# Moving the next group's first layer norm and step-size chain in among the matrix steps of a fused state-space and expert kernel

## The reference, cut to what matters

```python
x = x + attn(layernorm(x))     # a recurrence over the tokens, 4 heads
x = x + experts(layernorm(x))  # router, top 2 of 8 experts, and a shared one

# inside attn, for the tokens t in order:
dt    = clip(softplus(dt_raw + dt_bias), 1e-4, 0.1)
denom = 1 + dt * kdamp + dt**2 * A
v = (v - dt*A*y + dt*u*Bv) / denom
y = y + dt*v + dt*u*By
o = y . Cy + v . Cv
```

## Time and profile before

| what | us |
|---|---|
| median of 3 runs | 531.29 (530.99 to 531.33) |
| the profiled execution | 531.18 |
| its span, first to last instruction | 529.4 |
| DVE busy | 445.4 (84%) |
| PE busy | 446.4 (84%) |
| POOL busy | 282.7 (53%) |
| ACT busy | 242.6 (46%) |

### The profile page before, as it was taken

How to read it: one execution, slowest core, us unless ns; L and a number is a source line. 1 busy time by engine, 2 the same in 40 slices (tenths; PEclk the granted TensorE clock), 3 DMA queues, 4 the chain that set the end, 5 groups by cost and what they waited for, 6 DMA issues and landing times.

```text
span 529.4 us, 9508 instructions
## 1 busy us (share of the span) xinstructions
PE 446.4 (84%) x3185; PEld 344.8 (65%) x3185; DVE 445.4 (84%) x1268; ACT 242.6 (46%) x482; POOL 282.7 (53%) x367
## 2 busy tenths in 40 slices
PE   6980159996989989997889969898789969998997
PEld 5360158774756667675757659676656658876986
DVE  7699988968999999968999998968889998787542
ACT  1522227443475436442575526443466534343463
POOL 2007887656108876657108686567305776777000
PEclk9686559999999979999999988999899998998999
DMA  7500000200000001200000000110000000000000
GB/s 221 169 1 0 1 1 2 81 2 1 0 1 1 1 1 43 80 2 2 1 0 2 0 2 21 47 36 2 1 0 2 1 1 22 1 2 1 1 11 11
DMA packets 14794, 10.23 MB, mean 19 GB/s; under 512 B 1797, under 2 KB 13966, under 8 KB 14618
## 3 DMA queue, kind: packets, MB, share of 16 engines
q1 hardware_dynamic: 14746, 9.63, 6.2%
HBM read 8.55 MB, written 1.07 MB: 18 GB/s over the span
## 4 chain that ended last, share of the span: by engine, by line
DVE 41%; PE 37%; POOL 9%; issue 8%; ACT 3%; DMA 1%; SPq 0%; DVEq 0%; POOLq 0%; ACTq 0%
PE BC L612 6%; DVE tpA L1291 6%; DVE GV L1291 5%; DVE xr L1439 5%; PE HB L515 4%; DVE BC L1302 4%; PE GV L634 4%; POOL vt L1628 3%; PE HB L572 3%; PE HB L504 3%; POOL rinv L1663 2%; DVE mm L1339 2%; DVE GV L1302 2%; PE HB L622 2%; PE OO L693 2%
## 5 line engine op out<-in xcount | busy, mean ns | idle before, releaser
L612 PE MATMUL BC<-xnT,winT 128*128 128x128 f32 x512 | 78.8, 303 | 40.7 <-ACT pr L926 22.8
L612 PEld LDWEIGHTS BC<-xnT,winT 128*128 128x128 f32 x512 | 69.3, 211 | 54.1 <-issue 28.9
L1625 POOL TENSOR_TENSOR big<-mm 128x256 f32<-128x256 f32 x64 | 50.2, 784 | 52.3 <-DVE mm L1339 45.7
L1648 POOL TENSOR_SCALAR uT<-uT,skipT 128x512 f32<-128x512 f32 x8 | 12.5, 1570 | 89.3 <-DVE w L1424 53.9
L564 PE MATMUL HB<-xnT,w 128*128 128x512 f32 x108 | 52.0, 603 | 3.7 <-ACT gtm L1013 2.1
L1628 POOL TENSOR_TENSOR vt<-mm 128x256 f32<-128x256 f32 x64 | 53.9, 842 | 0.0
L634 PE MATMUL GV<-big,vt 128*128 128x128 f32 x256 | 44.0, 296 | 8.9 <-POOL vt L1628 8.9
L1637 POOL TENSOR_TENSOR mm<-ab,pr 128x256 f32<-128x256 f32 x48 | 41.4, 884 | 14.9 <-ACT pr L926 14.9
L950 ACT ACTIVATE big<-GV 128x256 f32<-128x256 f32 x60 | 23.1, 384 | 56.8 <-PE GV L637 55.5
L1337 DVE TENSOR_TENSOR mm<-BC,pr 128x512 f32<-128x512 f32 x64 | 44.2, 691 | 5.7
L634 PEld LDWEIGHTS GV<-big,vt 128*128 128x128 f32 x256 | 35.4, 200 | 16.8 <-POOL vt L1628 13.6
(11 more groups left out here) (212 smaller groups left out, 1117.1 us busy)
## 6 DMA issues: line engine op xcount, KB each, us to landing
ab<-dt_rows SPq DMA_DIRECT2D x12, 256.0 KB, 4.2
xr<-in_x SPq DMA_DIRECT2D x4, 256.0 KB, 4.9
winT<-in_w_inT SPq DMA_DIRECT2D x1, 1024.0 KB, 6.5
w<-in_rw SPq DMA_DIRECT2D x1, 1024.0 KB
out<-xr SPq DMA_DIRECT2D x3, 256.0 KB, 3.0
taps<-in_dw_wT SPq DMA_DIRECT2D x1, 512.0 KB, 3.8
w<-in_sw SPq DMA_DIRECT2D x2, 128.0 KB
out<-xr SPq DMA_DIRECT2D x2, 128.0 KB, 1.8
```

The costliest lines, as they stand in the source:

```text
L612: last = pe.matmul(b[:, j * TS:(j + 1) * TS], winT[:, col:col + NS], xt, start=True, stop=True)
L1625: pool.tensor_tensor(wt[q % 8][:], m[:, 0], m[:, 3], ALU.add)
```

## The change

The preparation of group g+1 up to dt squared leaves the head loop. On DVE it becomes `front_stage(g + 1, slot)`, called from `between`: one instruction (in two slots, two) at a time among the steps of group g. A dependent instruction takes its wait (`behind`) in its own slot. The other engines get their parts at fixed places between the experts. The rows and the four denominator products stand at the front of the head loop, in iterations 0, 1, 2 and 4 in place of 9, 10, 12 and 13. The running sums stay at 16 and 17. Group 0's own preparation, ahead of everything, stays as it was.

```diff
-DENS_AT = (9, 10, 12, 13)
+F_DENS, DENS_AT = (9, 10, 12, 13), (0, 1, 2, 4)
+SCANS_AT = (16, 17)
+S_STATS, S_AGGR, S_EPS, S_LOGITS, S_DT = 0, 4, 6, 32, 52
+XN_AFTER, XNT_AFTER, LOGITS_AFTER = 2, 3, 4
+DT_OPS = 12
...
 # tensor
+            norm_T(LN1, 1)
+            logits(1)
             pe.wait_ge(ab_done, 1)
...
             for g in range(NG):
+                if g + 1 < NG:
+                    rows_of_dt(g + 1)
                 for k in range(STEPS_OF[g]):
...
-                        front_early(g + 1, k)
+                        if k in DENS_AT:
+                            denominator(g + 1, DENS_AT.index(k))
...
                         hidden(g, e)
+                        if g + 2 < NG:
+                            if e == XNT_AFTER:
+                                norm_T(LN1, g + 2)
+                            if e == LOGITS_AFTER:
+                                logits(g + 2)
                         if e:
                             expert_out(g, e - 1)
...
 # scalar
             for n in range(CHUNKS):
                 convert(0, n)
+                if n == 0:
+                    norm1(1)
+                if n == 1:
+                    xnT_copy(1)
+                if n == 2:
+                    logits_copy(1)
+                if n == 4:
+                    step_exp(1)
             for g in range(NG):
+                if g + 1 < NG:
+                    rows_copy(g + 1)
...
                         for n, last in CONV_AFTER:
                             if e == last:
                                 convert(g + 1, n)
+                                if n == 5 and g + 2 < NG:
+                                    step_exp(g + 2)
+                        if g + 2 < NG:
+                            if e == XN_AFTER:
+                                norm1(g + 2)
+                            if e == XNT_AFTER:
+                                xnT_copy(g + 2)
+                            if e == LOGITS_AFTER:
+                                logits_copy(g + 2)
...
 # vector
+            def front_stage(g, slot):
+
+                if S_STATS <= slot < S_STATS + GT:
...
+                    ins = dve.bn_stats(stats[:, c, :], xr[g % 3][:, c, :])
...
+                if S_AGGR <= slot < S_AGGR + 2:
...
+                if slot == S_EPS:
+                    behind()
+                    dve.tensor_scalar(mv[:, :, 1], mv[:, :, 1], EPS_LN, None, ALU.add).then_inc(ln_var, 1)
+                if slot == S_LOGITS:
...
+                if slot == S_LOGITS + 2:
+                    behind()
+                    dve.tensor_scalar(lx, lx, 0.0, None, ALU.min).then_inc(dt_e, 1)
+                n = slot - S_DT
+                if n == 0:
+                    dve.wait_ge(dt_exp, g + 1)
+                    chained(dve.tensor_scalar(le, le, E_MAX, None, ALU.min))
...
 # gpsimd
             def fills(g):
-                skip_gate(g)
+                if g == 0:
+                    skip_gate(g)
+                if g + 1 < NG:
+                    scale_and_shift(ln_index(LN1, g + 1))
+                if g:
+                    skip_gate(g)
```

More of the change, by code:

```diff
@@ L477, in norm_T, with logits @@
                 last.then_inc(h_ready, 1)
-            def front_early(g, k):
+            def logits(g):
+                pe.wait_ge(h_free, h_read_of("xnT", g))
+                hb = h_bank("logits", g)
+                for c in range(GT):
+                    last = pe.matmul(hb[:, NH * c:NH * c + NH],
+                                     xnTs[g % 2][:, HALO + c * TS:HALO + (c + 1) * TS],
+                                     winT[:, COL_DT:COL_DT + NH], start=True, stop=True)
+                last.then_inc(h_ready, 1)
@@ new lines, in rows_of_dt, with denominator @@
+            def rows_of_dt(g):
+                pe.wait_ge(dt_done, g + 1)
+                hb = h_bank("rows", g)
+                for c in range(GT):
+                    last = pe.transpose(hb[0:2 * NH, c * TS:(c + 1) * TS],
+                                        dtts[g % 2][:, c].rearrange("p i h -> p (i h)"), ident[:])
+                last.then_inc(h_ready, 1)
+            def denominator(g, h):
+                pe.wait_ge(h_free, h_read_of("rows", g))
+                hb = h_bank("den", g, h)
+                pe.matmul(hb[:], coef8[:, h, :], rows8, start=True, stop=True).then_inc(h_ready, 1)
@@ L480, in front_early, with front_first @@
+            def front_first(k):
                 if k == F_XNT:
-                    norm_T(LN1, g)
+                    norm_T(LN1, 0)
                 if k == F_LOGITS:
[L484 to L489, removed]
@@ L490, in front_early @@
-                    last.then_inc(h_ready, 1)
-                if k == F_ROWS:
[L493 to L504, removed]
+                    logits(0)
@@ L834, in _, with norm1 @@
             by_tile = lambda t: t.rearrange("p (c t) -> p c t", c=GT)
[L836 to L846, removed]
-                if k == F_XNT:
[L848 to L854, removed]
+            def norm1(g):
+                act.wait_ge(ln_rstd, ln_index(LN1, g) + 1)
+                act.wait_ge(h_ready, USE[("xnT2", g - 2) if g >= 2 else ("xnT", g - 1)] + 1)
+                for c in range(GT):
+                    last = act.activation(xn[:, c, :], xr[g % 3][:, c, :], ACT.Identity, bias=shift[:, c:c + 1],
+                                          scale=rstd[:, c:c + 1])
+                last.then_inc(ln_xn, 1)
@@ L1028, in _ @@
             for k in range(MID_STEPS):
[L1029 removed]
+                front_first(k)
             head_powers()
@@ L1452, in between @@
                     add_expert(g - 1, e, c)
+                if g + 1 < NG and slot < 2 * DS:
+                    front_stage(g + 1, slot)
             dve.memset(ones[:], 1.0)
```

138 lines of the change are left out of this document (101 added, 37 removed).

## The result

The changed kernel takes 553.87 us (median of 6, 547.84 to 556.20) against 531.31 for the kernel before, measured beside it: a ratio of 1.0371, interval 1.0302 to 1.0441. I had forecast slower, but 537.0 with a range up to 543. The profiled execution has a span of 552.9 us and a mean granted clock of 0.901, against 529.4 and 0.932.

The account below looks back on a forecast made before the run. DVE was taken to bound group 1's steps, and PE, with DVE close behind, the head loops. Steps pay 18.6 us, loops gain 12.7: 5.9 more than 531.2 gives 537.1, stated as 537.0, range 533 to 542, whole range 527 to 543.

Parts of the forecast that it names:

- What the head loop gains: Head loops of groups 0 to 2: preparation leaving them gives back 1.7, 5.0 and 6.0 us, 12.7 in all.
- the 48 us that I had named as a sign of being wrong: Head loops: forecast near 46 us; one under 45 or over 48 would show the prediction wrong.
- ceiling of 47.4: Head loop: the last group's 44.2 us plus products 1 to 3 at 1.05 us each.
- PE's own sum: Head loop: PE busy 46.28 less 1.9, 44.4 us, plus some 1.5 of waiting, said to agree with 46.0.
- What the step stages pay: Steps of groups 0 to 2: slots, waiting and contention cost 4.6, 7.0 and 7.0 us, 18.6 in all.
- contention of DVE with POOL's fills: Steps: each chain instruction waits for a fill's end; 2.8 us for eight in group 0, 1.3 each in groups 1 and 2.
- wait at slot 52: Steps of groups 1 and 2: DVE waits 3.5 us for ACT's exponential, after PE idles 2.6 us before the transposes.
- rival 3: Step stage: PE's clock falls after the new 2.6 us gap, costing PE 3 us; two groups give 543; chance 0.10.
- The cover: Before pair 0: rows on PE and their copy on ACT cost nothing, hidden under DVE's own fill unless PE is slow.
- Rival 2: Steps: no wait at slot 52, as PE catches up or ACT's scale comes earlier; 530.1, or 524; chance 0.22.
- Rival 4: Both moves come out even: little contention in groups 1 and 2, wait near 1 us; 531 to 533; chance 0.11.
- Rival 5: Short DVE instructions in empty slots aren't free: 0.12 us for each of some 29, 3.5 in all; 540.6; chance 0.03.

Follow-up runs that it names:

- PE held busy: Changed kernel plus repeated products and identity transposes on PE in the two step-stage gaps and ahead of the rows, groups 1 and 2: 543.08 us, ratio 1.0161.
- spread: Changed kernel with the exponential ahead of conversion 5, normalising split behind experts 2, 3 and 4, transposes, logits, bias and clamp later: 544.16 us, ratio 1.0224.
- mended late kernel: Changed kernel with denominator products in iterations 9, 10, 12, 13, exponential ahead of conversion 5, normalising split, POOL's scale before skip_gate in group 0: 539.65 us, ratio 1.0133.
- products late: Changed kernel with the next group's four denominator products back in iterations 9, 10, 12 and 13: 542.44 us, ratio 1.0202.
- slot 51: Changed kernel with the chain of twelve one slot earlier, 51 in place of 52: 553.87 us in one run, no ratio.
- layer norm alone: Against the kernel before, only layer norm, transposes and logits moved among the steps, normalising split, POOL's scale first in group 0: 534.66 us, ratio 1.0033.

## Why the prediction was wrong

**The failed step is "What the head loop gains": 12.7 us.** The loops gave nothing; all three lie over the 48 us that I had named as a sign of being wrong. By its parts:
- I put product 0 in a gap and products 1 to 3 where "PE has about 2 us of work to DVE's 2 us", each at 1.05 us, and then took 46.0, under my own ceiling of 47.4. With PE held busy loops 1 and 2 take 47.46 and 47.64: the ceiling. Against the 46.0 that is 1.5 and 1.6. An iteration of 2.81 us there is PE's own work; there was no slack for the product. All of the cost lies in front: loop 1 takes 22.1 us from pair 0 to pair 8 and the last group's loop of that kernel 18.7, from pair 8 to pair 15 they take 25.4 and 25.2, so the 1.4 that I took off for iteration 9 did not come. And 3.3 us is also what the products cost at the back (14.79 us against 11.53 from pair 12 to pair 15): the new place saved nothing even with the clock up. What I called PE's own sum was off too: PE is busy for 42.55 us of this loop and not for 44.4, and idle for 5 and not for 1.5.
- The clock. I applied the doubled price of a product to group 0 alone, though loop 2 of the kernel before begins at half clock as well. A product costs 2.00 us there, and the stretch is no longer 6 us but 17 in loop 1 and 10 in loop 2. This costs 6.2 us in loop 1 (53.67 less 47.46) and 2.2 in loop 2. That the early products draw the stretch out is shown by all kernels together: in groups 1 and 2 the low clock at the loop's start takes 3.4 to 17.1 us behind pair 0 in sixteen loops with early products, over 9.9 in eleven of them, and 0.9 to 6.8 in ten with late ones. The spread and the mended late kernel, whose steps in group 1 are equal, differ by 4.5 in loop 1. But the 6.2 and 2.2 are those of one execution: in the six kernels with early products and nothing to hold PE, loops 1 and 2 took 47.36 to 53.67 us, 50.8 in the mean. In loop 0 the miss is 2.4, and it is the clock's too: the same code took 46.42 and 46.72 in two other kernels, where the clock came back 4.8 and 5.5 us behind pair 0 in place of 11.2.
- Sum of these: 1.5 + 1.6 + 6.2 + 2.2 + 2.4 = 13.9, which is 1.2 against -12.7.

**What the step stages pay: 18.6, measured 23.5.**
- Group 0: 4.6 forecast, 6.8 measured. The lock-out of 5.57 us is the difference; without it (products late, slot 51) the stage costs 4.2. The cause was right, contention of DVE with POOL's fills, but not its course: I had each instruction of the chain wait for the end of one fill, 0.78 us each, and instead the first waited through seven whole fills and those behind it took 0.16 to 0.17 us, as POOL was done. The course that I forecast is that of the five kernels without the lock-out (0.24 to 0.72 us each under the fills).
- Group 1: 7.0 forecast, 10.4 measured. The wait at slot 52 was 3.5 and is 3.3, behind a gap of PE of 2.28 us where I had 2.6; slots and contention were 2.2 + 1.3 = 3.5, and DVE is busy for 38.43 us instead of 35.02, 3.4 more. The missing 3.4 are rival 3: the clock fell after the new gap, which put expert 3 late by 1.56 us and rows and square by 2.56. Both waits are gone with PE held busy, and the stage is 4.0 us shorter.
- Group 2: 7.0 forecast, 6.3 measured, without a fall of the clock.

**The cover.** I had called the rows and their copy free under DVE's own fill and named a slow PE as what would take this away. It did, in group 1; in group 2 it held.

**The rivals.** Rival 2 is out: the wait at slot 52 is there in every kernel that has the chain in that slot, 1.11 us at the least. Rival 3 came true in one of its two groups, with its price of 3 us. Its fault, and mine, was to look for the low clock in the steps only. Rival 4 needed a wait near 1 us and is out with the 3.30 and 3.24. Rival 5 stays out: in the kernel with the layer norm alone nine instructions were added to group 0's steps and cost 0.4 us, where 0.12 for each is 1.1.

For this execution the account closes: 5.9 forecast, 13.9 and 4.9 missed, and -1.2 in tails, start and last group, is 23.5, the difference of the spans. My noise of 0.2% was too small: the kernel before alone lay between 530.10 and 535.23 in six executions, the changed one between 547.84 and 556.20.

**What stays open.** Why the clock stays low so long in most loops with early products and not in all, and what decides whether DVE gets its turn between two fills. No version with the change or a part of it was faster than the kernel before.

## What to carry to other kernels

Before moving work to the front of a loop, look at the granted clock there: price TensorE's instructions by what they cost at the level that the loop starts with, and ask whether they lie on the one engine that then paces it. A gap of 2 us that a reordering tears in PE's queue can cost more than the 2 us; filling such gaps with throw-away products gained 10.8 us here. A short DVE instruction is free only where it has an empty slot and POOL is idle: the same 16 elements cost 0.17 us alone, 0.2 to 0.9 under POOL's instructions as a rule, and 5.6 at worst. And moving work within the loop of the engine that paces it need not gain anything: the four products cost 3.3 us at the back and 3.3 at the front, before the clock.

## What the runs showed of the hardware

- The granted clock stayed at 0.50 while PE was busy for 9.98 of 10.00 us (195 to 205) and for 9.00 of 9.00 (216 to 225), that is at 1.2 GHz. The Trainium skill ("TensorE: Matmul & The Clock Gate", Part 1) ties the level to how busy PE has been; that an idle stretch comes ahead of the fall agrees with these rows, and that a busy one brings the clock back did not hold over these stretches.
- A DVE instruction of 16 elements was shut out through seven whole POOL instructions in a row, 5.57 to 5.61 us in five kernels, with one input and with two. The Trainium skill ("SBUF — State Buffer", SBUF: two separate sides) has the two engines exclude each other for one whole instruction. The times of 0.24 to 0.92 us, each of which ends as a POOL instruction ends, agree; the seven in a row go beyond it, and the measurement decides.
- The same gap in PE's queue had both outcomes: after 2.00 us of idling the clock fell in group 1 and not in group 2 of the changed kernel, after 1.27 us in group 2 and not in group 1 of the spread one. The changed kernel's runs spread over 8 us; that this is the reason is argued from it, not shown.
